# Later first load of Wo and fewer query matmuls ahead of the attention loop

## The chip, the cores and the metric

One core of a Trainium2 chip runs the whole program. The metric is the device time of one execution in microseconds; less is better. A time of several runs is their median.

## The reference

Eight batches of 256 tokens with 512 features go through a gated cross-attention block and a gated mixture-of-experts block:

```python
x = x + tanh(g_xattn[0]) * attention(layernorm(x), ctx_2048, Wq, Wk, Wv, Wsk, Wsv, Wo)
x = x + tanh(g_ffn[0]) * ffn(layernorm(x), router, gate, up, down, amplitudes, expert_scale, shared weights)
# attention: 32 query heads of 16 features, 8 key heads; q = concat(ctx, xn) @ Wq
# k = xn @ Wk and ctx @ Wsk, v likewise; both key sets are masked to a window of 64 positions
# o = softmax(q k^T / 4 + alibi) v, then o @ Wo
```

## The kernel before

Every matrix product is made of three passes, high x high, low x high and high x low, where each operand is split into a rounded part ("hi", made by ScalarE, ACT) and the rest ("lo", made by VectorE, DVE, or GpSimd, POOL). A weight half (128 x 512) arrives in a staging buffer, is rounded (`weights_high`, L1032), and its rest is formed (`weights_low`, L1403 on DVE, L847 on POOL). `wait_split` waits until both parts stand.

Ahead of the loop, TensorE (PE) does batch 0's keys, values and queries (`keys_values`, L1865; `first_queries`, L1896), turns the normalised rows (`prep`, L1845), then batch 1's keys and its first queries (`queries`, L1807). A query product `r` (0 to 3) of a batch has 24 matmuls of 128 x 256.

The loop over slots `n` is software-pipelined by a table of offsets written out by hand. 32 slots make one batch (8 groups of 4 windows). In slot `n`, PE computes the scores of unit `n` (L1921), DVE their maxima (L1448), PE turns the maxima after each 8 slots, and 18 slots later PE computes the scores turned (L1948), ACT their exponentials (L1099). Products with v (L1962), the scaling by POOL (L816), two 32 x 32 transposes by DVE (L1466, L1475) and `o_high` / `o_low` (L1110, L822) bring the attention output to `OT`, which meets `WO` from slot 56 on. Between these, PE gets pieces of later batches' projections.

Queries and keys reach the stacked operands `QS` and `KS` by DMA. Keys are written to DRAM (`keep_k`, L580) and read back (`stack_k`, L596). Queries either go straight from SBUF to SBUF in three DMAs of 64 KB a group (`stack_q_direct`, L603; batches 0, 1 and 7), or to DRAM (`keep_q`, L586) and back in one DMA of 192 KB a group (L619). All of these are issued by the one in-order SP queue, and each slot's waits in it stand in the way of what follows. `scores(4g)` waits for the stacks of group `g`.

SP's order ahead of its loop is: weights and rows, `load_ctx(1)`, `load_x(2)`, `keep_k(0)`, the four loads of Wo (L562), the stacks of batch 0 for eight groups, `keep_k(1)`. `Q1` holds batch 1's queries, in SBUF that the normalised rows `X1N` and the turned rows `XS` use later; Wo is staged where `OT` lies later. The later user of each place waits for the earlier one.

Of the kernel before, what the change touches and what calls it, by code (L numbers as in the profile page):

```python
# [80 lines left out]
LOAD_ROWS, STATS = -61, (-51, -50)  # L81
# [5 lines left out]
EARLY_Q = ((-1, -1, 7), (-1, -1, 8), (9, 10, 11), (12, 13, 14))  # L87
PIECES = 8
# [6 lines left out]
SPLIT_WO = 12  # L95
FIRST_STACK, WARM = 16 * (1 + PARTS), 7
TANH, LOAD_GATES = 54, 44
# [77 lines left out]
def projections():  # L175


    order = [("k", 0, 0), ("v", 0, 0)] + [("q", 0, r) for r in range(G)] + [("k", 1, 0), ("q", 1, 0), ("q", 1, 1)]
# [19 lines left out]
def build(nc, a, out):  # L198
# [27 lines left out]
    wo_stage = at("wo_stage", 184 * KIB, [P, HC, HID])  # L226
    OT = {h: at(f"oT_{h}", (184 + n * 4) * KIB, [P, TB, HC, P], F32R) for n, h in enumerate(("hi", "lo"))}
    Q1 = {h: at(f"second_qT_{h}", (216 - n * 8) * KIB, [P, NB, 2, G, HQ], F32R) for n, h in enumerate(("hi", "lo"))}
# [152 lines left out]
    def staging(n):  # L381
        if n >= FIRST_O:
            return wo_stage[:, n - FIRST_O, :]
        return stage[:, n % 8, :]
# [55 lines left out]
    def straight(b):  # L440


        return b in (1, B - 1)

    def q_loads(b):


        return 16 * sum(PARTS if straight(i) else 1 for i in range(1, b + 1))
# [102 lines left out]
    def _(sp):  # L551
# [60 lines left out]
        def stack_q(b, g):  # L612
            sp.wait_ge(st_mm, (b - 1) * UNITS + NB * (g + 1))
            if straight(b):
# [3 lines left out]
            sp.wait_ge(q_kept, 16 * PARTS * (b - 1))  # L618
# [21 lines left out]
        for n in range(FIRST_O, len(halves)):  # L640
            weight(n)
# [5 lines left out]
        keep_k(1)  # L647
        for n in range(SLOTS):
# [22 lines left out]
            if b is not None:  # L671
# [3 lines left out]
                else:  # L675
                    sp.wait_ge(prep_t, 2 * TB)
# [14 lines left out]
            if s == STACKED[HK - 1] + 2:  # L691
                for g in range(HK):
                    sp.wait_ge(q_in[g], q_loads(B - 1))
# [75 lines left out]
    def _(pool):  # L769
# [259 lines left out]
    def _(act):  # L1029
# [73 lines left out]
        def o_high(p):  # L1103
# [4 lines left out]
            elif c == 0:  # L1108
                wait_split(act, len(halves) - 1)
# [679 lines left out]
    def _(pe):  # L1789
# [476 lines left out]
```

## Time and profile before

| | us |
|---|---|
| median of 3 runs | 892.43 |
| the three runs | 886.06, 892.43, 1215.84 |
| the profiled execution (the last of these values) | 1215.84 |
| its span, first to last instruction | 1213.9 |
| mean granted TensorE clock in it | 0.655 |

The profiled execution is the longest of the three: 323 us above the median. Its span leaves 1.9 us outside. In the profile a share of 99% for PE says that some matmul was always under way, at the clock that was granted; it does not say that PE would be as full at a higher clock.

### The profile page before, as it was taken

The numbers are of one execution on the slowest core, as the hardware profiler recorded it, in microseconds if no ns is written. First come the engines' busy times: TensorE is split into PE (matmuls) and PEld (weight loads), VectorE is DVE, ScalarE is ACT, GpSimd is POOL, SyncE is SP. The second block draws the span as 40 slices with busy tenths as digits, with TensorE's granted clock in tenths as the row PEclk, the third lists the DMA queues.
The fourth block names the chain that finished last, engine by engine and source line by source line (L and its number), as shares of the span: only waits on it lengthen the run. The fifth ranks groups of instructions, "written<-read, shape, count | busy, mean of one in ns | idle before, by whom it ended". The sixth has DMA issues, their size and how long they took to land.

```text
span 1213.9 us, 17380 instructions
## 1 busy us (share of the span) xinstructions
PE 1205.9 (99%) x6662; PEld 910.6 (75%) x6662; DVE 541.2 (45%) x983; ACT 404.0 (33%) x810; POOL 487.1 (40%) x526
## 2 busy tenths in 40 slices
PE   9999999999999999999999999999999999999998
PEld 9999898989898998766666656666666666666665
DVE  6554545554555446311254353434344434443445
ACT  5543343433343335430231223222322233222321
POOL 4532332323223203414484523444555455555320
PEclk7666666666666666666666666666666666666666
DMA  7734454535454336601010333110101101010034
GB/s 236 161 90 118 125 159 118 165 112 166 116 143 144 97 97 163 214 1 35 18 35 18 113 123 131 35 53 18 53 18 53 52 18 52 28 60 18 1 120 158
DMA packets 77947, 110.17 MB, mean 91 GB/s; under 512 B 7329, under 2 KB 49058, under 8 KB 76834
## 3 DMA queue, kind: packets, MB, share of 16 engines
q1 hardware_dynamic: 75656, 108.04, 30.6%
q10 hardware_dynamic: 2210, 1.03, 0.4%
q8 instruction: 53, 0.87, 0.3%
q14 instruction: 28, 0.23, 0.1%
HBM read 71.76 MB, written 32.05 MB: 86 GB/s over the span
## 4 chain that ended last, share of the span: by engine, by line
PE 98%; DVE 1%; issue 0%; ACT 0%; POOL 0%; POOLq 0%
PE ps_scores L2162 21%; PE ps_proj L1807 14%; PE ps_scoresT L2162 10%; PE ps_scoresT L1948 7%; PE ps_proj L1796 7%; PE ps_scores L1796 6%; PE ps_o L1962 6%; PE ps_scores L1921 5%; PE ps_scoresT L1796 5%; PE ps_proj L2162 5%; PE ps_proj L1865 5%; PE ps_o_max L1980 1%; PE ps_o_max L1845 1%; PE ps_scoresT L1896 1%; PE ps_o_max L1796 1%; PE ps_scores L1896 1%
## 5 line engine op out<-in xcount | busy, mean ns | idle before, releaser
L1448 DVE TENSOR_REDUCE neg_max<-ps_scores 128x2 f32<-128x384 f32 (+1 forms) x256 | 132.0, 518 | 218.2 <-PE ps_scores L1921 217.8
L1099 ACT ACTIVATE probsT<-ps_scoresT 128x512 f32<-128x512 f32 (+1 forms) x256 | 138.4, 544 | 248.8 <-PE ps_scoresT L1948 244.3
L1315 ACT ACTIVATE part_sums<-ps_scores 128x512 f32<-128x512 f32 x96 | 57.4, 598 | 232.5 <-PE ps_scores L2162 232.5
L1948 PE MATMUL ps_scoresT<-q_stack,k_stack 116*128 116x256 f32 x448 | 127.5, 358 | 1.3 <-ACT probsT L1099 1.3
L1921 PE MATMUL ps_scores<-k_stack,q_stack 114*128 114x192 f32 (+1 forms) x512 | 115.4, 312 | 1.1 <-DVE neg_max L1448 0.7
L1921 PEld LDWEIGHTS ps_scores<-k_stack,q_stack 114*128 114x128 f32 x512 | 106.1, 248 | 12.4 <-DVE neg_max L1448 2.4
L962 POOL TENSOR_TENSOR w_expert_lo<-w_sums,w_expert_hi 128x256 fp32r<-128x256 f32 x64 | 61.6, 972 | 105.4 <-ACT w_expert_hi L1238 105.4
L816 POOL TENSOR_TENSOR o_normal<-o_blocks,inv_sums 128x256 f32<-128x256 f32 x32 | 19.9, 621 | 201.5 <-DVE inv_sums L1469 201.5
L1948 PEld LDWEIGHTS ps_scoresT<-q_stack,k_stack 116*128 116x128 f32 x448 | 93.5, 249 | 6.9 <-issue 2.3
L974 POOL TENSOR_TENSOR big<-big,basis 128x512 f32<-128x512 f32 x56 | 71.6, 1288 | 41.2 <-DVE basis L1746 41.2
L1962 PE MATMUL ps_o<-probsT,v_ones 128*32 128x128 f32 (+1 forms) x2048 | 77.0, 324 | 0.0
L1807 PE MATMUL ps_proj<-actT_hi,wq_hi 128*128 128x256 f32 x224 | 76.2, 340 | 0.4 <-DVE second_qT_lo L1425 0.4
L1807 PE MATMUL ps_proj<-actT_hi,wq_lo 128*128 128x256 f32 x224 | 76.1, 340 | 0.0
L1807 PE MATMUL ps_proj<-actT_lo,wq_hi 128*128 128x256 f32 x224 | 75.4, 336 | 0.0
L1716 DVE TENSOR_TENSOR part_sums<-part_sums,ps_scoresT 128x512 f32<-128x512 f32 x32 | 22.0, 687 | 114.9 <-ACT part_sums L1315 114.9
L1962 PEld LDWEIGHTS ps_o<-probsT,v_ones 128*32 128x32 f32 x2048 | 64.3, 130 | 11.1 <-issue 0.8
L1737 DVE TENSOR_TENSOR basis<-part_sums,silu_gate 128x512 f32<-128x512 f32 x32 | 22.2, 693 | 106.3 <-ACT silu_gate L1323 106.3
L962 POOL TENSOR_TENSOR w_expert_lo<-w_raw,w_expert_hi 128x256 fp32r<-128x256 f32 x48 | 38.5, 815 | 76.5 <-ACT w_expert_hi L1238 76.5
L822 POOL TENSOR_TENSOR oT_lo<-oT_raw,oT_hi 128x256 fp32r<-128x256 f32 x32 | 23.5, 733 | 113.1 <-ACT oT_hi L1110 113.1
L2162 PE MATMUL ps_scores<-sum_lo,w_expert_hi 128*128 128x512 f32 x128 | 65.1, 508 | 0.0
L2162 PE MATMUL ps_scores<-sum_hi,w_expert_hi 128*128 128x512 f32 x128 | 65.1, 508 | 0.0
L2162 PE MATMUL ps_scores<-sum_hi,w_expert_lo 128*128 128x512 f32 x128 | 65.0, 508 | 0.0
(302 smaller groups left out, 2856.5 us busy)
## 6 DMA issues: line engine op xcount, KB each, us to landing
k_stack<-k_kept SPq DMA_DIRECT2D x64, 192.0 KB, 3.9
big<-coeff_rows SPq DMA_DIRECT2D x8, 1024.0 KB, 4.7
q_stack<-q_kept SPq DMA_DIRECT2D x40, 192.0 KB, 3.9
q_kept<-qT_hi SPq DMA_DIRECT2D x10, 512.0 KB
x_rows<-in_x SPq DMA_DIRECT2D x9, 512.0 KB, 4.8
k_kept<-kT_hi SPq DMA_DIRECT2D x16, 256.0 KB
x_kept<-x_rows SPq DMA_DIRECT2D x16, 256.0 KB, 2.0
w_raw<-in_L_ffn_w_gate SPq DMA_DIRECT2D x16, 256.0 KB, 2.9
```

The source lines that it names most:

```text
L962: pool.tensor_tensor(WS[n % 2]["lo"][:, w, :], w_source(n, w), WS[n % 2]["hi"][:, w, :].bitcast(F32), ALU.subtract).then_inc(e_lo, 1)
L974: pool.tensor_tensor(dst, dst, BS[:, j, :], ALU.add).then_inc(acc_done, 1)
L1099: act.activation(PT[:, g % 2, 2 * j:2 * j + blocks].rearrange("p h f r w -> p (h f r w)"), ST[:, n % 2, 0:blocks].rearrange("p h n -> p (h ...
L1315: act.activation(TP[:, u % 2, j, :], src[:, u % 2, :], ACT.Copy).then_inc(taken, 1)
L1448: dve.tensor_reduce(NM[:, g // 2 % 2, g % 2, 2 * i:2 * i + 2], SA[:, n % 2, :, 0:keys], AX.X, ALU.max, negate=True).then_inc(max_done, 1)
L1796: ins = pe.matmul(out, stat(s, c), mov(m, c), start=c == cs[0] and j == 0, stop=c == cs[-1] and j == PARTS - 1)
L1807: ins = pe.matmul(out, stat(s, c), mov(m, c), start=i == 0, stop=i == len(steps) - 1, skip_group_check=True)
L1865: ins = pe.matmul(dst[:, src * T:(src + 1) * T], WKV[w][:, m + src, c, :], AT[x][:, src * HC + c, :], start=i == 0, stop=i == HC * PARTS - ...
L1921: ins = pe.matmul(SA[:, n % 2, f, 0:2 * (near.stop - near.start)], QS[0:TOP, g, i, f].rearrange("p r w -> p (r w)"), keys[:, near, :].rear ...
L1948: ins = pe.matmul(ST[:, n % 2, v, :], KS[0:ROWS, g, j + v, 1 - v].rearrange("p w s -> p (w s)"), QS[0:ROWS, g, j + v].rearrange("p f r w - ...
L1962: ins = pe.matmul(POB[32 * r:32 * r + 2 * D, n % 2, j * W:j * W + cols_j], VA[:, j, n % HK, :], PT[:, n % 2, 2 * j:2 * j + cols_j // W, :, ...
L2162: ins = pe.matmul(bank[:, u % 2, :], WS[n % 2][s][:, w, c * P:(c + 1) * P], operand(MEETS[w], m, c, g), start=first and c == 0 and j == 0, ...
```

## The change

- Wo: its four loads leave the place ahead of batch 0's stacks. They are issued at slots 24 and 28, into `X1` and a small buffer; the splits move from slots 12 to 15 to slots 34 to 37 (ACT and POOL). The reload of `X1` at slot 42 waits for the split of the first two.
- Batch 1's queries: product 0 has half of its matmuls ahead of the loop (all 24 before) and the rest in slots 1, 3, 5 and 7, three each; product 1 moves from slots 0 to 7 (three each) to slots 9 to 11; products 2 and 3 start at 11 and 13 instead of 9 and 12.
- `Q1` moves to where `OT` lies later. So `o_high` of the first pair (slot 32) waits for the DMAs that read `Q1`, and POOL's first `x1_normalise` no longer does.
- Batch 1's queries go through DRAM for groups 2 to 7 (three writes of 512 KB by `keep_q(1)`, then one read a group), straight only for groups 0 and 1.
- `first_queries` waits for both parts of a weight half and does the three passes of a product in a row, instead of starting on the rounded part and going over the four products in each pass.
- Rows and context of batches 3 to 7 are loaded 3 slots earlier, the gates 6 slots earlier, the tanh 4 slots earlier.

```diff
-LOAD_ROWS, STATS = -61, (-51, -50)
+LOAD_ROWS, STATS = -64, (-51, -50)
-EARLY_Q = ((-1, -1, 7), (-1, -1, 8), (9, 10, 11), (12, 13, 14))
-PIECES = 8
+EARLY_Q = ((-1, -1, 7), (9, 10, 11), (11, 12, 13), (13, 14, 15))
+DIRECT = 2
+EARLY_PIECES = {1: 4, 3: 5, 5: 6, 7: 7}
-SPLIT_WO = 12
+LOAD_WO, SPLIT_WO = (24, 28), 34
-TANH, LOAD_GATES = 54, 44
+TANH, LOAD_GATES = 50, 38
...
-    wo_stage = at("wo_stage", 184 * KIB, [P, HC, HID])
+    wo_stage = at("wo_stage", 216 * KIB, [P, 2, HID])
-    Q1 = {h: at(f"second_qT_{h}", (216 - n * 8) * KIB, ...
+    Q1 = {h: at(f"second_qT_{h}", (184 + n * 4) * KIB, ...
...
-            return wo_stage[:, n - FIRST_O, :]
+            return (X1, wo_stage)[(n - FIRST_O) // 2][:, (n - FIRST_O) % 2, :]
...
-        return b in (1, B - 1)
+        return b == B - 1 or (b == 1 and g < DIRECT)
...
+            if n == FIRST_O:
+                sp.wait_ge(prep_t, 2 * TB)
...
-            sp.wait_ge(q_kept, 16 * PARTS * (b - 1))
+            sp.wait_ge(q_kept, 16 * PARTS * b)
...
         keep_k(0)
-        for n in range(FIRST_O, len(halves)):
-            weight(n)
         for g in range(HK):
             stack_k(0, g)
             stack_q_first(g)
             if g == 4:
                 load_ctx(2)
         keep_k(1)
+        keep_q(1)
...
+            if n in LOAD_WO:
+                for m in range(2):
+                    weight(FIRST_O + 2 * LOAD_WO.index(n) + m)
...
                 else:
-                    sp.wait_ge(prep_t, 2 * TB)
+                    wait_split(sp, FIRST_O + 1)
                 sp.dma_start(X1[:], x_t[:, b]).then_inc(x1_in, 16)
...
-            elif t == 0:
-                for g in range(HK):
-                    pool.wait_ge(q_in[g], q_loads(1))
...
             elif c == 0:
-                wait_split(act, len(halves) - 1)
+                act.wait_ge(q_kept, 16 * PARTS)
+                for g in range(DIRECT):
+                    act.wait_ge(q_in[g], q_loads(1, g))
...
             for c in cs:
-                for j, (w, m) in enumerate((("hi", "hi"), ("hi", "lo"), ("lo", "hi"))):
-                    if j == 0:
-                        pe.wait_ge(weights_hi, HALF_Q[c] + 1)
-                    elif w == "lo":
-                        wait_split(pe, HALF_Q[c])
-                    for r in range(G):
+                wait_split(pe, HALF_Q[c])
+                for r in range(G):
+                    for j, (w, m) in enumerate(PASSES):
...
         queries(1, 0, 0, 2)
         keys_values("k", 1, 1)
-        queries(1, 0, 1, 2)
...
-            if n < PIECES:
-                queries(1, 1, n, PIECES)
+            if n in EARLY_PIECES:
+                queries(1, 0, EARLY_PIECES[n], 8)
```

## Rows read from the trace of the kernel before

**Rows 1.** The page: span, busy time and share of each engine.

```profile
span 1213.9 us, 17380 instructions
PE 1205.9 (99%) x6662; PEld 910.6 (75%) x6662; DVE 541.2 (45%) x983; ACT 404.0 (33%) x810; POOL 487.1 (40%) x526
```

**Rows 2.** Windows: engines' busy us (instructions), granted clock, DMA share, GB/s.

```profile
3.00:4.00 1.00, 1.00 (x4) 0.82 (x3) 0.00 (x0) 0.58 (x1) 0.00 (x0) 1.00 0.98 309
6.00:7.00 1.00, 0.94 (x3) 0.26 (x1) 1.00 (x3) 0.60 (x2) 0.00 (x0) 0.65 1.04 365
...
0.00:41.00 41.00, 39.82 (x223) 37.95 (x223) 23.26 (x43) 22.05 (x41) 24.41 (x34) 0.70 0.71 214
41.00:560.00 519.00, 515.45 (x4440) 462.31 (x4439) 249.19 (x564) 204.86 (x421) 147.10 (x193) 0.65 0.47 125
```

**Rows 3.** Waits of PE over the whole span, two of six kinds: us, times, longest.

```profile
PE ps_scoresT L1948 <- ACT probsT L1099: 1.3, 4, 0.4
...
PE ps_proj L1807 <- DVE second_qT_lo L1425: 0.4, 1, 0.4
```

**Rows 4.** The chain that ended last, in order of time, 35 to 41 us.

```profile
35.33 1.95 PE ps_proj L1807 x12
37.27 1.94 PE ps_proj L1865 x12
39.21 2.00 PE ps_proj L1807 x12
```

**Rows 5.** SP's queue in order of time, 24 to 72 us.

```profile
24.37 0.60 SPq L580 DMA_DIRECT2D k_kept<-kT_lo  x1
25.02 3.49 SPq L562 DMA_DIRECT2D wo_stage<-in_L_xattn_Wo  x4
31.42 0.65 SPq L596 DMA_DIRECT2D k_stack<-k_kept  x1
33.46 0.62 SPq L603 DMA_DIRECT2D q_stack<-qT_hi  x1
...
35.45 0.57 SPq L596 DMA_DIRECT2D k_stack<-k_kept  x1
...
52.62 0.57 SPq L596 DMA_DIRECT2D k_stack<-k_kept  x1
...
71.19 0.57 SPq L596 DMA_DIRECT2D k_stack<-k_kept  x1
```

**Rows 6.** DMA issues by kind: count, KB each, median us to landing.

```profile
xT_kept<-xs_hi SPq DMA_DIRECT2D x5, 512.0 KB, 3.1
...
q_stack<-qT_hi SPq DMA_DIRECT2D x32, 64.0 KB, 3.2
wo_stage<-in_L_xattn_Wo SPq DMA_DIRECT2D x4, 256.0 KB, 6.2
```

**Rows 7.** PE in order of time at the loop's start and in slot 9.

```profile
41.00 0.40 PE L1921 MATMUL ps_scores<-k_stack,q_stack 114*128 114x128 f32 x2
...
48.88 0.38 PE L1807 MATMUL ps_proj<-actT_hi,wq_hi 128*128 128x256 f32 x1 [0.38 <-DVE second_qT_lo L1425]
```

**Rows 8.** Groups of instructions between 7 and 41 us.

```profile
L1403 DVE TENSOR_TENSOR wq_lo<-w_stage,wq_hi 128x512 fp32r<-128x512 f32 x8 | 5.3, 684 | 0.7 <-ACT wq_hi L1032 0.7
```

**Rows 9.** The splits of Wo: engine, count, duration min/median/max.

```profile
L1032 ACT ACTIVATE wo_hi<-wo_stage x4: 619/622/623, 54.0 to 58.9; 128x512 fp32r<-128x512 f32 x4
L847 POOL TENSOR_TENSOR wo_lo<-wo_stage,wo_hi x4: 1274/1280/1283, 54.8 to 65.0; 128x512 fp32r<-128x512 f32 x4
```

**Rows 10.** ACT in order of time around slots 32 to 35.

```profile
80.97 0.41 ACT L1110 ACTIVATE oT_hi<-oT_raw 128x256 fp32r<-128x256 f32 x1
...
86.72 0.60 ACT L1099 ACTIVATE probsT<-ps_scoresT 128x512 f32<-128x512 f32 x1 [2.40 <-PE ps_scoresT L1948]
```

**Rows 11.** POOL in order of time, slot 35.

```profile
88.61 0.62 POOL L816 TENSOR_TENSOR o_normal<-o_blocks,inv_sums 128x256 f32<-128x256 f32 x1 [6.42 <-DVE inv_sums L1469]
```

**Rows 12.** DVE in order of time: slot 1, then slot 37.

```profile
42.28 0.56 DVE L1448 TENSOR_REDUCE neg_max<-ps_scores 128x2 f32<-128x384 f32 x1 [0.42 <-PE ps_scores L1921]
...
91.42 0.44 DVE L1475 STREAM_TRANSPOSE oT_raw<-o_normal 128x256 f32<-128x256 f32 x1
```

More of the change, by code:

```diff
@@ L175, in projections @@
 def projections():
-    order = [("k", 0, 0), ("v", 0, 0)] + [("q", 0, r) for r in range(G)] + [("k", 1, 0), ("q", 1, 0), ("q", 1, 1)]
+    order = [("k", 0, 0), ("v", 0, 0)] + [("q", 0, r) for r in range(G)] + [("k", 1, 0), ("q", 1, 0)]
     for n in range(SLOTS):
@@ L225, in build @@
     stage = at("w_stage", 168 * KIB, [P, 8, HID])
-    wo_stage = at("wo_stage", 184 * KIB, [P, HC, HID])
+    wo_stage = at("wo_stage", 216 * KIB, [P, 2, HID])
     OT = {h: at(f"oT_{h}", (184 + n * 4) * KIB, [P, TB, HC, P], F32R) for n, h in enumerate(("hi", "lo"))}
-    Q1 = {h: at(f"second_qT_{h}", (216 - n * 8) * KIB, [P, NB, 2, G, HQ], F32R) for n, h in enumerate(("hi", "lo"))}
+    Q1 = {h: at(f"second_qT_{h}", (184 + n * 4) * KIB, [P, NB, 2, G, HQ], F32R) for n, h in enumerate(("hi", "lo"))}
     OB = at("o_blocks", 192 * KIB, [P, 2, T // 32, 2 * D])
@@ L438, in queries_of, with straight, q_loads @@
         return Q1 if b == 1 else Q
-    def straight(b):
-        return b in (1, B - 1)
-    def q_loads(b):
-        return 16 * sum(PARTS if straight(i) else 1 for i in range(1, b + 1))
+    def straight(b, g):
+        return b == B - 1 or (b == 1 and g < DIRECT)
+    def q_loads(b, g):
+        return 16 * sum(PARTS if straight(i, g) else 1 for i in range(1, b + 1))
     def wait_rows(eng, g):
@@ L613, in stack_q @@
             sp.wait_ge(st_mm, (b - 1) * UNITS + NB * (g + 1))
-            if straight(b):
+            if straight(b, g):
                 sp.wait_ge(pj_done, passed("q", b, G - 1))
@@ L692, in _ @@
                 for g in range(HK):
-                    sp.wait_ge(q_in[g], q_loads(B - 1))
+                    sp.wait_ge(q_in[g], q_loads(B - 1, g))
                 router = cols(a["L0_ffn_w_router"], 0)
@@ L1077, in q_high @@
             elif b >= 3 and r == 0:
-                act.wait_ge(q_kept, 16 * PARTS * (b - 2))
+                act.wait_ge(q_kept, 16 * PARTS * (b - 1))
             act.wait_ge(q_mm, G * b + r + 1)
@@ L1889, in first_queries @@
             for c in cs:
-                for j, (w, m) in enumerate((("hi", "hi"), ("hi", "lo"), ("lo", "hi"))):
-                    if j == 0:
-                        pe.wait_ge(weights_hi, HALF_Q[c] + 1)
-                    elif w == "lo":
-                        wait_split(pe, HALF_Q[c])
-                    for r in range(G):
+                wait_split(pe, HALF_Q[c])
+                for r in range(G):
+                    for j, (w, m) in enumerate(PASSES):
                         ins = pe.matmul(place("q", 0, r)[:, 0:T], WQ[w][:, c, r * P:(r + 1) * P], AT[m][:, c, :],
-                                        start=c == 0 and j == 0, stop=c == 2 * HC - 1 and j == PARTS - 1,
-                                        skip_group_check=True)
-                        if c == 2 * HC - 1 and j == PARTS - 1:
-                            ins.then_inc(q_mm, 1)
+                                        start=c == 0 and j == 0, stop=c == 2 * HC - 1 and j == PARTS - 1)
+                    if c == 2 * HC - 1:
+                        ins.then_inc(q_mm, 1)
         def turn_v(b):
@@ L1914, in scores @@
                 if b >= 1:
-                    pe.wait_ge(q_in[g], q_loads(b))
+                    pe.wait_ge(q_in[g], q_loads(b, g))
             if n >= 2:
@@ L2073, in _ @@
                     b = queries_due(n, r, part)
-                    if b is not None and (b > 1 or r > 1):
+                    if b is not None and (b, r) != (1, 0):
                         queries(b, r, part)
```

## The prediction

> **What bounds the kernel now.** I read the page's busy times first, then the windows with the granted clock, then PE's waits, and only then the timelines of the first 95 us, where the change works. PE is busy 1205.9 of 1213.9 us [rows 1]. The clock was granted in full at 3 to 4 us and at 0.65, between the two levels of 1.2 and 2.4 GHz, from 6 us on, and it stayed there through the loop [rows 2]. PE's waits inside the loop are counted in tenths of a microsecond [rows 3]. So this execution is bound by matmuls at 0.65 of the clock, and every supply chain hides behind them.
>
> The median run is another matter. The profiled execution is 1215.84 us, the other two are 886.06 and 892.43, and the median is the latter. PE's work scaled to a full clock is an estimate of 1205.9 x 0.655 = 790 us. A run of 889 us (the mean of those two) is then one of two things: PE at the full clock with some 99 us of waits that the profile doesn't show, or PE always full at 790 / 889 = 0.89 of the clock. I keep both readings. In either, PE's stretches shrink to 0.655 or 0.74 of what the profile shows, while DMA, ACT, DVE and POOL keep their durations. What is slack here may be a wait there.
>
> **The change part by part.**
>
> *Matmuls.* None is added or removed. Twelve go from ahead of the loop into it: 12 for 2.00 us at the profile's clock [rows 4], so 1.3 us at full clock.
>
> *Wo's loads.* After the last write of K (issued until 24.97) SP issues four loads for 3.49 us, and the first stack of keys, which waits for K to land, goes out at 31.42, 6.4 us after K's last issue. Group 0's queries follow at 33.46, when they are evicted [rows 5]. Wo's 1 MB lands in 6.2 us a piece [rows 6] and shares the DMA engines with K's write. Without it a write of comparable size lands in 3.1 us [rows 6], so K lands about 3.3 us earlier; the bounds are 0 (the write was slow by itself) and 3.9 us, to the time at which nothing but a landing of 2.5 us were left. By the Trainium skill, DMA: Bandwidth & Descriptors, Anatomy of one DMA, a DMA costs about 2.0 us plus its bytes over 436 GB/s; for 768 KB that is an estimate of 3.8 us, and the gain by it would be 2.6 us. In the profiled execution none of this shows, because group 0's stacks land at about 35.4 + 3.2 = 38.6 and PE comes to the loop at 41.00 [rows 5 to 7]. Scaled to the full clock it does: I estimate from the same rows that the first queries end near 26 us, K lands near 28.7, group 0's last query DMA is issued near 31.3 and lands near 34.5, while PE has filler only to about 33. So PE waits about 1.5 us at the loop's start before the change. After it, K lands near 25.5, the queries' eviction near 27 becomes the late one (the last product is then the only one left to evict, since each is finished in turn), and the stacks land near 32, with PE's filler ending at 31.7. The loop starts 2.3 us earlier.
>
> *The moved matmuls in the loop.* From its start the loop is bound in that scaled reading by SP: eight groups take 52.62 - 31.42 = 21.2 us to issue, 2.8 to 3.0 us a group [rows 5], and four slots of scores with three matmuls each take 3.3 us at the profile's clock and 2.2 at full. The 12 added matmuls find this gap and cost 0; with the gap gone they cost 1.3 us. A slot of scores alone is held by its maximum, 0.56 us [rows 12], so even slots without filler lose up to 0.2 us each, 4 x 0.2 = 0.8 us. I take 0.3 for both together.
>
> *Order of the first queries.* Each half now waits for its lo part, 0.68 us later than the hi part [rows 8]; eight halves bound it at 5.5 us, and 0 is the other bound. PE afterwards waits for DVE's rows and splits anyway, which the order doesn't move, so I take 0 to 0.5, and 0.2 for the sum. At the profile's clock it is 0: PE arrives later than the lo parts.
>
> *Waits in the slots 32 to 37.* The Wo splits are 4 x 0.62 us on ACT and 4 x 1.28 us on POOL [rows 9]. In slots 12 to 15 nothing hung on them. In slots 34 to 37 ACT has its exponentials, and behind POOL's first two splits stands the scaling of the second pair, 0.62 us at 88.61 [rows 11], for which DVE waits at 91.42 [rows 12], with the maxima queued behind it, and PE's scores behind those. From ACT's 86.72 + 0.60 [rows 10], a chain of 0.62 + 2 x 1.28 + 0.62 = 3.8 us ends at 91.1 in the profile, just in time. The distance to 91.42 shrinks from 4.1 us to 2.7 to 3.0 at the higher clock, so DVE would be late by about 1 us, and the two score buffers take some of it: 0.6 us, bounds 0 and 2.5. Before that, `o_high` at 80.97 [rows 10] waits for group 1's direct queries: they are released at 71.19 [rows 5], need 2.5 us of issue and 3.2 us to land [rows 6], so about 77; at the higher clock the 9.8 us shrink to 6.4 and the 5.8 do not. No wait, bound 1 us.
>
> *The rest.* `keep_q(1)` adds 1.5 MB of writes and stands on SP behind nothing urgent: the next entry of the queue is slot 22. Six groups then need one DMA in place of three, which frees SP by 12 x 0.58 us in slots 30 to 50; PE waits for none of them before, so it is worth 0. Were `keep_q(1)` late, group 2 at slot 30 would be the first to feel it, ten slots ahead of its use. Loading rows and context 3 slots earlier, the gates and the tanh: their consumers wait for nothing in the profile, 0. PE's only wait for an early query, 0.38 us in slot 9 [rows 7], goes, but product 2 in slot 11 takes the bank of product 0, which is now finished in slot 7: 0.
>
> The sum: -2.3 + 0.3 + 0.2 + 0.6 = -1.2 us. At the profiled execution's own clock the sum is 0 + 0.3 - 0.4 = 0, so 1215.8 again. Against the other two runs, whose mean is 889.2, it gives 888.0. This is below what a measurement of this kernel can tell: the two runs differ by 0.7% and I take 2% as the line between a change and none.
>
> **The rivals.**
>
> *More is gained.* In the shorter runs the first 50 us may be paced by SP and the DMA engines throughout: the share is 0.71 over the first 41 us even with PE at 0.65 [rows 2]. Then Wo's 3.49 us of issue and its 6.2 us in the engines come off whole, about 9.7 us: 879. Against it: DVE's chain and PE's own work stand beside it.
>
> *It does nothing.* If PE is full at 0.89 of the clock, slack covers the stacks nearly everywhere, and the time is 889 give or take 1.
>
> *Slower by blocked splits.* POOL's four splits in slots 34 to 37, 5.1 us, and ACT's 2.5 us delay the output chain and with it DVE and PE. It is dearer than the early gain if more than 2.9 us of it reach PE. The whole of 7.6 us would give 889.2 - 1.7 + 7.6 = 895.1. For it speaks the bare 0.3 us of margin at the profile's clock; against it that it occurs once, not in each batch.
>
> *The clock.* Slots 0 to 8 become sparser in matmuls. In the profile the clock fell to 0.65 while PE was busy and did not rise again [rows 2], so it follows something other than idle time there. If it halved for the roughly 5 us of these slots, the cost is 5 us: 893. The Trainium skill (TensorE: Matmul & The Clock Gate, HAM oscillation) has idle gaps bring the half rate; no row here shows that.
>
> **How the numbers follow.** Forecast 0.56; more gained 0.10; nothing 0.16; slower by splits 0.14; clock 0.04. The predicted time is 888. The range reaches down to 886.06 less the 8 us of most of the larger gain, 878, and up to 892.43 plus the full 7.6 us, 900. Faster by over 2% would need 17.8 us, more than all terms together: 0.03. Slower by over 2%: 0.03. Within: 0.94.
>
> **What would show it.** Right: the last K write and the first stack of keys lie about 3 us apart instead of 6.4, the first scores start 2 us earlier in the profile (39 against 41.00), the maxima in slots 0 to 8 stand closer together than 0.8 us, DVE's transpose in slot 37 shows an idle time ended by POOL, and PE's share stays at 98 or 99% at any clock of 0.65. Wrong: a PE wait of several microseconds at a score or a turned score after slot 34, or K's write still at 6 us. A clock that differs from run to run would move the time more than all of this.

## The result and the profile after

The changed kernel takes 894.47 us (median of 7 runs, 892.60 to 894.64), the kernel before 888.65 us (median of 7). The ratio is 1.0058, its 95% interval 1.0035 to 1.0081: slower by 5 to 6 us, inside 2%, and resolved all the same. The ratios leave out the executions of the kernel before that ran far longer at a low mean clock (1215.84 us here, 1067.66 and 1422.68 us beside e0 to e3). The forecast was 888.0 us in 878 to 900. The range held the time; the direction was wrong.

The profile of before stood at a clock of 0.655. A second profile of the unchanged kernel, taken on the chip of the first experiments, was granted the full clock (885.15 us, span 883.2) and is the base of every comparison below; the profiled execution of after took 892.44 us. The page after (the first row answers to [rows 1]):

```profile
span 890.4 us, 17369 instructions
PE 872.0 (98%) x6662; PEld 758.9 (85%) x6662; DVE 539.8 (61%) x983; ACT 400.1 (45%) x810; POOL 509.9 (57%) x526
```

At nearly the full clock PE is still busy 98% of the span, 872 us, not the 790 us that the prediction scaled to. So PE is nearly full at either clock, and time is won or lost in the few places where PE stops or its clock is halved. They are found by the start of the same slot's scores in the two traces. The table is worked out from the first matmul of L1921 in each slot: the first row is the time in us in the second profile of before, each other row the distance to it. Experiments are named by their number.

```
slot            0      8     16     30     34     36     96    232    240   span
before      34.62  40.54  49.23  63.45  69.48  73.20 158.90 352.35 359.82  883.2
after       -2.22  -1.73  +1.73  +1.27  +2.18  +3.74  +3.74  +3.74  +7.09  890.4
e1          -2.16  -3.27  -0.70  -1.13  +2.83  +3.02  +3.02  +3.02  +6.58  889.9
e2          -1.26  -2.45  -1.91  -1.89  +4.60  +4.65  +4.65  +4.65  +6.10  890.7
e3          -1.13  -1.91  +0.33  -0.12  +5.94  +5.95  +5.94  +5.95  +7.39  890.8
e4          -1.15  -2.61  -0.09  -0.52  +4.45  +4.59  +4.59  +4.60  +8.12  891.4
e5          +0.84  +1.23  +1.23  +1.25  +1.26  +1.26  +1.26  +1.28  +4.63  887.9
e6          -1.02  -0.66  +1.28  +0.86  +6.39  +6.48  +7.33  +7.34 +10.24  893.5
e7          +0.49  +0.57  +0.57  +0.58  +9.11  +9.11  +9.11  +9.13 +10.57  893.9
e8          -0.74  -1.92  -1.40  -1.31  +1.87  +1.90  +1.90  +1.91  +1.94  885.2
e9          -1.23  -2.17  -1.88  +1.21  +1.22  +1.22  +1.22  +1.23  +1.24  884.6
e10         -1.78  -2.90  -0.62  +0.18  +0.22  +0.25  +1.10  +1.11  +1.11  884.5
e11         -1.80  -2.49  -0.14  +0.08  +0.33  +0.33  +0.33  +0.34  +3.16  886.5
e12         +0.87  +1.26  +1.25  +1.24  +1.25  +1.25  +1.25  +3.02  +3.07  886.4
e13         +0.76  +0.60  +0.37  +0.37  +0.37  +0.37  +0.37  +4.38  +5.83  891.4
e14         -1.62  -2.33  -0.40  -0.85  +4.16  +4.23  +4.23  +6.00  +6.05  889.3
e15         -1.26  -2.18  +0.11  -0.32  +6.03  +6.54  +6.55 +10.56 +12.01  897.8
```

Each row is one execution, and rows that should be alike show how far one can be trusted. Up to slot 101 e12 and e13 are the kernel before, and they come to the loop 0.87 and 0.76 us later than the base. Up to slot 24 e1, e4, e6, e14 and e15 do the same work as after: they start between -2.16 and -1.02 (after: -2.22) and stand between -1.13 and +0.86 at slot 30 (after: +1.27). A difference of up to 1.2 us at slot 0, or 2.4 us at slot 30, between two single rows shows nothing by itself. Nor is the profiled execution always the typical one: that of e8 is the fastest of its 13, those of e5 and e15 are the slowest of 12 and 5.

The row of after reads: 2.2 us won at the loop's start; 3.5 us lost in slots 8 to 16; 2.5 us lost in slots 30 to 36; then nothing at all for 196 slots; and 3.35 us lost between slots 232 and 240, in the last batch, whose work the change doesn't touch.

**The start.** SP's queue, the kernel before (full clock), then after (both answer to [rows 5]; columns are start, duration, queue and line, operation):

```profile
22.11 0.61 SPq L580 DMA_DIRECT2D k_kept<-kT_lo  x1
22.77 3.80 SPq L562 DMA_DIRECT2D wo_stage<-in_L_xattn_Wo  x4
29.43 0.65 SPq L596 DMA_DIRECT2D k_stack<-k_kept  x1
30.18 0.62 SPq L603 DMA_DIRECT2D q_stack<-qT_hi  x1
```

```profile
21.81 0.61 SPq L583 DMA_DIRECT2D k_kept<-kT_lo  x1
27.46 0.64 SPq L599 DMA_DIRECT2D k_stack<-k_kept  x1
28.20 0.62 SPq L606 DMA_DIRECT2D q_stack<-qT_hi  x1
```

From the end of K's last issue (22.72, 22.42) to the first stack of keys it is 6.7 us before and 5.0 us after. So Wo's loads had cost K's write 1.7 us, about half of the 3.3 us taken. This figure is steady: 6.7 to 7.1 us in the five profiles that have the loads there, 4.9 to 5.1 us in the twelve that don't. PE comes to the loop 2.2 us earlier all the same, in these two profiles and by the means of like ones (35.2 us in e0, e5, e7, e12 and e13; 33.0 us in after, e1, e4, e6, e14 and e15).

**Slots 30 to 36.** SP's queue in after, from `keep_q(1)` on:

```profile
52.25 0.75 SPq L589 DMA_DIRECT2D q_kept<-second_qT_hi  x1
53.04 0.57 SPq L589 DMA_DIRECT2D q_kept<-second_qT_lo  x1
53.66 0.65 SPq L589 DMA_DIRECT2D q_kept<-second_qT_hi  x1
58.03 0.59 SPq L599 DMA_DIRECT2D k_stack<-k_kept  x1
59.13 0.66 SPq L606 DMA_DIRECT2D q_stack<-second_qT_hi  x1
59.84 1.35 SPq L606 DMA_DIRECT2D q_stack<-second_qT_lo  x1
61.23 2.21 SPq L606 DMA_DIRECT2D q_stack<-second_qT_hi  x1
63.55 1.24 SPq L565 DMA_DIRECT2D x_rows<-in_L_xattn_Wo  x2
64.89 0.57 SPq L599 DMA_DIRECT2D k_stack<-k_kept  x1
65.56 0.55 SPq L606 DMA_DIRECT2D q_stack<-second_qT_hi  x1
66.16 0.58 SPq L606 DMA_DIRECT2D q_stack<-second_qT_lo  x1
66.79 0.58 SPq L606 DMA_DIRECT2D q_stack<-second_qT_hi  x1
67.41 1.05 SPq L565 DMA_DIRECT2D wo_stage<-in_L_xattn_Wo  x2
```

The three writes are issued in 2 us. Behind them stand batch 1's first stacks, and they are late in two ways. The issues of queries take 0.66, 1.35 and 2.21 us for the first group here. In the second profile of before they take 0.58 us each for the first group, and once 1.23 us for the second:

```profile
60.70 0.58 SPq L603 DMA_DIRECT2D q_stack<-second_qT_hi  x1
61.34 0.58 SPq L603 DMA_DIRECT2D q_stack<-second_qT_lo  x1
61.96 0.58 SPq L603 DMA_DIRECT2D q_stack<-second_qT_hi  x1
...
63.94 1.23 SPq L603 DMA_DIRECT2D q_stack<-second_qT_lo  x1
```

And they land late. The landing rows of the tile `q_stack` between 58 and 69 us are, of before:

```profile
DMA to landing us min/median/max: 2.3/3.0/4.4
```

(as in [rows 6]) and of after:

```profile
DMA to landing us min/median/max: 4.8/6.1/7.5
```

The keys' stacks go from a median of 3.9 to 8.1 us in the same windows. Group 1's last read closes at 73.4, and `o_high` hangs on it, with an exponential behind it and a product with v behind that. ACT in time, then the chain that ended last:

```profile
69.53 0.60 ACT L1101 ACTIVATE probsT<-ps_scoresT 128x512 f32<-128x512 f32 x1 [2.39 <-PE ps_scoresT L1948]
73.52 0.42 ACT L1114 ACTIVATE oT_hi<-oT_raw 128x256 fp32r<-128x256 f32 x1 [3.40 <-DMA q_stack<-second_qT_hi]
73.84 0.37 ACT L1101 ACTIVATE probsT<-ps_scoresT 128x256 f32<-128x256 f32 x1
```

```profile
66.79 6.63 DMA q_stack<-second_qT_hi
...
73.52 0.10 ACT oT_hi L1114
...
73.84 0.38 ACT probsT L1101
...
74.26 0.97 PE ps_o L1962 x32
```

In the second profile of before `oT_hi` stands at 67.85 with no wait at all, as in [rows 10].

**The clock.** Windows, of before at full clock, then of after (columns: window, its length, busy us and instructions of PE, PEld, DVE, ACT, POOL; granted clock, DMA share, GB/s; they answer to [rows 2]):

```profile
35.00:40.00 5.00, 4.09 (x35) 3.88 (x35) 3.29 (x7) 4.97 (x11) 5.00 (x6) 1.00 0.66 141
70.00:75.00 5.00, 5.00 (x94) 4.91 (x87) 2.84 (x6) 2.14 (x4) 0.62 (x1) 1.00 0.61 142
350.00:355.00 5.00, 3.84 (x58) 3.50 (x62) 3.66 (x10) 3.24 (x8) 4.04 (x4) 1.00 0.91 242
355.00:360.00 5.00, 4.71 (x71) 4.06 (x59) 3.81 (x9) 3.48 (x8) 0.62 (x1) 1.00 1.02 241
```

```profile
35.00:40.00 5.00, 3.79 (x24) 3.21 (x24) 3.37 (x10) 4.84 (x10) 4.91 (x6) 0.88 0.60 116
40.00:45.00 5.00, 5.00 (x35) 5.00 (x35) 2.73 (x7) 0.27 (x1) 0.00 (x0) 0.78 0.85 224
70.00:75.00 5.00, 3.67 (x79) 3.41 (x80) 1.19 (x3) 1.50 (x5) 0.73 (x1) 1.00 1.07 208
355.00:360.00 5.00, 3.55 (x22) 3.15 (x26) 3.71 (x8) 2.76 (x7) 2.77 (x3) 0.63 0.77 198
360.00:365.00 5.00, 4.95 (x77) 4.33 (x70) 2.22 (x5) 1.46 (x3) 0.00 (x0) 0.69 0.74 186
```

Taken in steps of 1 us, after spends 3.4 us at half clock (1.2 GHz) from 38 to 43 us and 6.8 us from 356 to 364; the second profile of before spends none. What PE did before the first fall: two waits, 0.66 us for a maximum at 34.13 and 1.21 us for group 1's first queries at 36.65. Slots 8 to 16 have this fall in them, and the moved matmuls: PE does 72 query matmuls between the scores of slots 8 and 16, 48 in the kernel before, and 12 instead of 24 between those of slots 0 and 8 (both are taken apart below).

### The profile page after: what moved, and what is told of

The parts are those of the page before. It is cut to its first block, busy times and chain, and to the rows that moved or that the text cites. A ratio compares the mean times of both kernels' runs of the same rounds, so it can differ in the third digit from the quotient of the medians.

```text
span 890.4 us, 17369 instructions
## 1 busy us (share of the span) xinstructions
PE 872.0 (98%) x6662; PEld 758.9 (85%) x6662; DVE 539.8 (61%) x983; ACT 400.1 (45%) x810; POOL 509.9 (57%) x526
## 4 chain that ended last, share of the span: by engine, by line
PE 89%; DVE 3%; DMA 3%; issue 1%; SPq 1%; POOL 1%; ACT 1%; DVEq 0%; POOLq 0%; ACTq 0%
PE ps_scores L2161 20%; PE ps_proj L1811 13%; PE ps_scoresT L2161 10%; PE ps_scoresT L1948 6%; PE ps_scores L1800 6%; PE ps_o L1962 6%; PE ps_proj L1800 5%; PE ps_scores L1921 5%; PE ps_scoresT L1800 5%; PE ps_proj L2161 5%; PE ps_proj L1869 4%; DMA xn_rows<-in_x 1%; DMA q_stack<-second_qT_hi 1%; DVE neg_max L1452 1%; PE ps_o_max L1980 1%
## 5 line engine op out<-in xcount | busy, mean ns | idle before, releaser
L1948 PE MATMUL ps_scoresT<-q_stack,k_stack 116*128 116x256 f32 x448 | 106.8, 311 | 1.7 <-ACT probsT L1101 1.6
L1921 PE MATMUL ps_scores<-k_stack,q_stack 114*128 114x192 f32 (+1 forms) x512 | 97.1, 273 | 6.0 <-DVE neg_max L1452 4.0
L1921 PEld LDWEIGHTS ps_scores<-k_stack,q_stack 114*128 114x128 f32 x512 | 82.6, 193 | 13.5 <-DVE neg_max L1452 4.7
L1948 PEld LDWEIGHTS ps_scoresT<-q_stack,k_stack 116*128 116x128 f32 x448 | 70.5, 192 | 6.4 <-ACT probsT L1101 2.8
L1811 PE MATMUL ps_proj<-actT_hi,wq_lo 128*128 128x256 f32 x224 | 63.4, 284 | 0.0
L1962 PE MATMUL ps_o<-probsT,v_ones 128*32 128x128 f32 (+1 forms) x2048 | 57.5, 265 | 1.3 <-ACT probsT L1101 1.3
L1750 DVE TENSOR_TENSOR basis<-basis,big 128x512 f32<-128x512 f32 x56 | 56.8, 1015 | 1.0
L1962 PEld LDWEIGHTS ps_o<-probsT,v_ones 128*32 128x32 f32 x2048 | 51.8, 112 | 5.2 <-ACT probsT L1101 1.5
L2161 PE MATMUL ps_scores<-xnT_hi,w_expert_hi 128*128 128x512 f32 x128 | 49.8, 389 | 0.0
L2161 PE MATMUL ps_scores<-xnT_hi,w_expert_lo 128*128 128x512 f32 x128 | 49.8, 389 | 0.0
```

The source lines that it names most:

```text
L1750: dve.tensor_tensor(dst, BS[:, j, :], cB[:, k % 2, group_columns(t)], ALU.mult).then_inc(basis_done, 1)
L1811: ins = pe.matmul(out, stat(s, c), mov(m, c), start=i == 0, stop=i == len(steps) - 1, skip_group_check=True)
L1921: ins = pe.matmul(SA[:, n % 2, f, 0:2 * (near.stop - near.start)], QS[0:TOP, g, i, f].rearrange("p r w -> p (r w)"), keys[:, near, :].rear ...
L1948: ins = pe.matmul(ST[:, n % 2, v, :], KS[0:ROWS, g, j + v, 1 - v].rearrange("p w s -> p (w s)"), QS[0:ROWS, g, j + v].rearrange("p f r w - ...
L1962: ins = pe.matmul(POB[32 * r:32 * r + 2 * D, n % 2, j * W:j * W + cols_j], VA[:, j, n % HK, :], PT[:, n % 2, 2 * j:2 * j + cols_j // W, :, ...
L2161: ins = pe.matmul(bank[:, u % 2, :], WS[n % 2][s][:, w, c * P:(c + 1) * P], operand(MEETS[w], m, c, g), start=first and c == 0 and j == 0, ...
```

## The experiments

Four jobs, each a set of runs on one chip: e0 to e3; e5 to e8; e4 with e9 to e11; e12 to e15. Each ratio is to runs of the kernel before in the same job.

**e0: the kernel before, unchanged.** 

> The kernel before, unchanged, to have its profile at a clock near the 0.994 at which the changed kernel was profiled. Expected 886 to 891 us. Theory (the wait for group 1's direct queries is the loss): in slots 24 to 32 ACT's first oT_hi waits for no DMA, and the stretch from the first score to slot 40 is 3 to 5 us shorter than in the changed kernel. Rival (the loss is at the loop's start): the first score of slot 8 is reached earlier than 38.9 us. Third possibility (the steady batches lose through the earlier loads of rows): the loss builds up evenly, batch by batch.

885.15 us, clock 1.000. It is the base described above.

**e1: one direct group instead of two.**

```diff
-DIRECT = 2
+DIRECT = 1
```

> The changed kernel with only group 0 of batch 1 stacked straight from SBUF, so that the first oT_hi in slot 32 waits for a DMA released four slots earlier. Theory (that wait costs 3 to 5 us): 0.4 to 0.6% faster than the changed kernel, so a ratio to before of 1.000 to 1.002, and oT_hi's wait of 3.4 us on the DMA is gone. Rivals (loop start, or rows loaded earlier, or splits in slots 34 to 37): ratio to before stays at 1.005 to 1.007.

893.09 us, 1.0056 [1.0034, 1.0078]: as slow as the change. `o_high`'s wait is gone, and PE now waits for the same jam at a score, in the waits of PE from 60 to 85 us:

```profile
PE ps_scores L1921 <- DMA k_stack<-k_kept: 2.4, 1, 2.4
```

So the wait of `o_high` was the last to end, but a stack of batch 1 stood right behind it.

**e2: batch 1's early query products as before.**

```diff
-EARLY_Q = ((-1, -1, 7), (9, 10, 11), (11, 12, 13), (13, 14, 15))
-EARLY_PIECES = {1: 4, 3: 5, 5: 6, 7: 7}
+EARLY_Q = ((-1, -1, 7), (-1, -1, 8), (9, 10, 11), (12, 13, 14))
+PIECES = 8
...
```

> The changed kernel with the early query matmuls where the kernel before has them. Theory of the DMA wait in slot 32: the ratio to before stays at 1.004 to 1.007. Rival that the matmuls moved out of slots 0 to 7 leave PE idle there: 0.2 to 0.5% faster than the changed kernel, a ratio of 1.001 to 1.004.

893.74 us, 1.0070 [1.0048, 1.0092]. At slot 30 it is 0.8 us ahead of e1 (-1.89 against -1.13) and 1.0 to 2.8 us ahead of e4, e6, e14 and e15, so the moved matmuls cost 0.8 us at the least. All of it, and more, is lost at slot 32, where PE waits 3.9 us for `k_stack`.

**e3: the order of the first queries as before** (three passes over four products, starting on the rounded part).

> The changed kernel with the first queries in the order of before (starts on the hi part, passes outermost). Theory of the DMA wait: the ratio to before stays at 1.004 to 1.007. Rival that waiting for the lo parts delays the start: 0.1 to 0.2% faster than the changed kernel. By my forecast's term (0.2 us) nothing measurable; it could also be slower by 0.1%, since the four evictions then come together.

893.88 us, 1.0066 [1.0046, 1.0086]. The loop starts at -1.13. That is 1.1 us behind after, but inside the -2.22 to -1.02 of the six profiles that have the new order, so no gain or cost of the order is shown. PE waits 3.6 us for `k_stack` at slot 32, ACT 2.4 us for the direct reads.

**e4: rows and context loaded 3 slots later, as before.**

```diff
-LOAD_ROWS, STATS = -64, (-51, -50)
+LOAD_ROWS, STATS = -61, (-51, -50)
```

> The changed kernel with the rows and contexts loaded at their old slots. In the steady batches the distance to before is constant, so I expect no effect there. Batch 3's rows and context no longer join the queue at slot 32: if that adds to the jam, the ratio falls by 0.001 to 0.002; else it stays at 1.004 to 1.007.

893.25 us, 1.0047 [1.0021, 1.0073]; the wait at slot 32 is still 2.4 us for `k_stack`. In e4 and in after the distance is constant from slot 36 to 232, with late and with early loads: they are worth nothing, as forecast.

**e5: the kernel before with only the new order of the first queries.**

> The kernel before with only the new order of the first queries. Theory (each product ends in turn, so three of its four evictions are done when the last one ends, and the first stacks leave SP earlier): the first score comes 1.0 to 1.2 us earlier than the 34.62 us of before, the time falls by 1 us at equal mean clock, a ratio of 0.997 to 1.000. My forecast's term (waiting for the lo parts costs 0.2 us): the first score 0 to 0.3 us later and a ratio of 1.000 to 1.002.

887.72 us, 0.9995 [0.9976, 1.0014]. It gains nothing. The loop starts at +0.84, but so it does at +0.87 and +0.76 in e12 and e13, whose order is that of before; the order's effect is smaller than this spread.

**e6: the changed kernel with Wo's loads past the stacks of groups 0 and 1.**

```diff
-LOAD_WO, SPLIT_WO = (24, 28), 34
+LOAD_WO, SPLIT_WO = (36, 38), 42
```

> The changed kernel with the loads of Wo at slots 36 and 38 and their splits at 42 to 45. Theory A (Wo's 1 MB in slots 24 to 28 is what makes the stacks of slot 32 late): the waits for DMA around slot 32 fall below 0.5 us and slot 40 lies 3 us earlier relative to before than in the changed kernel; ratio 0.999 to 1.003. Theory B (the 1.5 MB that keep_q(1) writes in slots 17 to 20 block the SP queue and the DMA engines): a wait of 1.5 to 4 us at slot 32 stays, and the ratio is 1.004 to 1.006. Both together: the wait is halved.

893.18 us, 1.0066 [1.0040, 1.0092]. With Wo's 1 MB out of the way PE still waits 2.9 us for `k_stack` at slot 32. The theory that Wo's loads jam the stacks falls. Another 0.85 us goes between slots 36 and 96, where the loads and splits of Wo now lie; e10, which has two of the loads and splits there, loses as much.

**e7: the kernel before, plus the writes of `keep_q(1)`, which nothing reads.** Direct reads of all groups stay; the counts of `q_kept` move by one batch, and POOL's first reuse of `Q1`'s place waits for the writes too.

```diff
...
         keep_k(1)
+        keep_q(1)
...
```

> The kernel before plus the three writes of batch 1's queries to DRAM, which nothing reads; the stacks stay straight. It doubles the suspected cost alone. Theory B: SP's issues of batch 1's first stacks take over 1 us each in place of 0.58, PE or ACT waits 1 us or more for a stack at slot 32, the clock falls there in some runs, and the time is 2 to 5 us above before (1.002 to 1.005). Theory A: nothing over 1 us at slot 32, ratio 1.000 to 1.002.

896.43 us, 1.0100 [1.0076, 1.0125]. The jam appears in the kernel before, and stronger. SP's queue, PE in time, and the landings of `q_stack` from 58 to 69 us:

```profile
57.93 2.67 SPq L586 DMA_DIRECT2D q_kept<-second_qT_hi  x1
...
62.19 1.46 SPq L603 DMA_DIRECT2D q_stack<-second_qT_hi  x1
63.70 2.39 SPq L603 DMA_DIRECT2D q_stack<-second_qT_lo  x1
66.14 1.90 SPq L603 DMA_DIRECT2D q_stack<-second_qT_hi  x1
```

```profile
73.63 0.66 PE L1923 MATMUL ps_scores<-k_stack,q_stack 114*128 114x128 f32 x2 [6.19 <-issue]
```

```profile
DMA to landing us min/median/max: 3.8/6.5/7.4
```

The profile names no releaser for the 6.19 us, but the instruction is `scores(32)`, the first that needs group 0 of batch 1. Between slots 30 and 36 8.5 us are lost, part of them at half clock (71 to 79 us).

**e10: the changed kernel without `keep_q(1)`.** All groups read `Q1` directly, so it stays at its old place, and Wo comes through `X1` in two pairs (loads at slots 24 and 36, splits at 34, 35, 42, 43).

```diff
-DIRECT = 2
+DIRECT = HK
-LOAD_WO, SPLIT_WO = (24, 28), 34
+LOAD_WO, SPLIT_AT = (24, 36), {34: 12, 35: 13, 42: 14, 43: 15}
...
-        keep_q(1)
```

> The changed kernel without the writes of keep_q(1): batch 1's queries lie at their old place and all eight groups are stacked straight; Wo is loaded in two pairs into X1 at slots 24 and 36, split at 34, 35, 42, 43. If those writes are what costs the time at slot 32, no wait for a stack is left there and slot 64 is 2 to 4 us earlier than in the changed kernel, level with before or up to 1 us later: ratio 0.999 to 1.003. If Wo's loads or the splits in slots 34 to 37 cost it, the ratio stays above 1.004.

888.31 us, 1.0007 [0.9987, 1.0026], level with before. There is no wait for a stack at slot 32; the landings of `q_stack` from 58 to 69 us are nearly those of before, and the first three issues of queries take 0.59, 0.59 and 0.52 us:

```profile
DMA to landing us min/median/max: 2.2/3.7/4.5
```

The rest of the change is in it, and it gains nothing either: -1.78 at slot 0 is +0.14 by slot 20. Of this 1.9 us go between slots 12 and 16, as in every profile with the moved matmuls and in none without them (PE has 40 query matmuls there in place of 24), and 0.8 us by slot 20, where PE waits 0.96 us for the queries of group 5 of batch 0.

**e8: the kernel before with the new order of first queries, Wo's loads moved behind batch 0's stacks** (still ahead of `keep_k(1)`; splits at slots 24 to 27).

```diff
-        for n in range(FIRST_O, len(halves)):
-            weight(n)
         for g in range(HK):
...
+        for n in range(FIRST_O, len(halves)):
+            weight(n)
         keep_k(1)
```

> The kernel before, with the new order of the first queries and with the four loads of Wo moved behind the first stacks (ahead of keep_k(1)), split in slots 24 to 27; batch 1's queries stay straight from their old place, so no writes are added. If the early gain is real and the loss lies in the added traffic of slots 17 to 28, the first score comes 1.3 us earlier than in before, slot 30 2.5 us earlier, and slot 64 still 2 us earlier: 2 us faster at equal clock, ratio 0.995 to 0.999. If Wo's loads disturb wherever they lie near slot 32, slot 64 is level with before or later.

891.14 us, 1.0041 [1.0025, 1.0057]. It leads by 1.3 us at slot 30 and loses 3.2 us there: POOL's splits of Wo stand in front of the low part of the turned context, and PE waits for it and for two exponentials behind it; the clock is halved from 66 to 70 us. The profile is of the fastest execution, 887.20 us at a mean clock of 0.998; the other twelve took 890.56 to 892.37 us at 0.990 to 0.994, so a good part of what the median lost isn't in it (waits of PE, 60 to 85 us):

```profile
PE ps_scoresT L1944 <- ACT probsT L1099: 1.2, 2, 0.9
PE ps_proj L1865 <- POOL actT_lo L809: 1.1, 1, 1.1
```

**e9: e8 with one load of Wo behind each stack of groups 3 to 6, splits at 18.**

```diff
...
+            if 3 <= g < 7:
+                weight(FIRST_O + g - 3)
...
```

> As e8, with the four loads of Wo set between the stacks of groups 3 to 6 and the splits in slots 18 to 21, clear of POOL's work in slots 27 and 28. In e8 slot 30 was 2.2 us ahead of before and slot 34 0.5 us behind, with POOL's context low part 1.1 us late and the splits ahead of it. If the splits' place was the reason, slot 64 stays 1.5 to 2.5 us ahead: 2 us faster at equal clock, ratio 0.996 to 0.999. If not, the loss at slots 31 to 34 stays, ratio 1.000 to 1.004.

887.83 us, 0.9996 [0.9978, 1.0014]. The lead of 1.87 us at slot 24 is gone by 28, in a wait of 1.17 us for DVE's maxima and a half clock from 58 to 62 us.

**e11: e9 with the moved query matmuls.** 

> As e9, with the early query matmuls where the changed kernel has them. From the changed kernel with them undone (slot 30 was 2.7 us ahead of before in place of 1.1 or less) I expect the first score 1 us earlier than in e9 but slot 30 1 to 2 us later, and PE idle in slots 0 to 7: ratio 0.001 to 0.003 above e9.

886.94 us, 0.9993 [0.9977, 1.0009]. The moved matmuls cost 1.3 us by slot 24 (-0.57 against -1.87); by the medians it is no slower than e9.

Then what was left: why does the last batch lose 3.35 us, and only in some runs? In the second profile of before PE waits there for the same maxima (2.7 us in all from 345 to 370 us, the longest 1.1) and stays at full clock. Two theories: it depends on where in time the batch falls (P), or on what the changed kernel did early (H). Extra matmuls at slot 101, in the full part of the loop, shift everything behind them and touch nothing else (they write scores that the following matmul overwrites).

```diff
-            for f in range(2):
+            for f in (0,) * (16 if n == 101 else 0) + (0, 1):
```

**e12: before, 16 extra.** 

> The kernel before with 16 extra matmuls in slot 101 (each writes the scores' half again that the next one overwrites, so nothing else changes); a pair of them takes about 0.2 us, so everything behind shifts by 1.6 us. Theory P (position: the half clock in the last batch hangs only on where that batch falls in the run): the last batch falls to half clock in some or most runs, mean clock 0.994 to 0.998, time before + 1.6 + up to 3.3 us. Theory H (history: it hangs on what the changed kernel does early): clock as in the kernel before in the same job, time + 1.6 us.

889.17 us, 1.0011 [0.9993, 1.0029]; shift 1.77 us, last batch +0.05, clock 0.996 to 1.0 in ten runs.

**e13: before, 36 extra.** 

> The kernel before with 36 extra matmuls in slot 101, a shift of 3.6 us, the size of the changed kernel's distance there (3.74). Theory P: half clock in the last batch as in the changed kernel, time + 3.6 + 3.3 = 6.9 us at a mean clock near 0.994. Theory H: clock as before, time + 3.6 us.

893.30 us, 1.0051 [1.0035, 1.0067]; shift 4.01 us, last batch +1.45 by slot 240 and 1.4 us more by slot 255, clock 0.995 to 1.0.

**e14: after, 16 extra.** 

> The changed kernel with the same 16 extra matmuls. Theory P: the last batch falls at another place, so its half clock may go: time + 1.6 - 3.3 us against the changed kernel. Theory H: half clock stays, time + 1.6 us, mean clock 0.992 to 0.994.

893.62 us, 1.0066 [1.0043, 1.0088]; last batch +0.05, clock 0.990 to 0.998. It does 1.8 us more work than after and its median isn't above after's 894.47, but its ten runs spread from 891.39 to 900.28.

**e15: after, 36 extra.** 

> The changed kernel with the same 36 extra matmuls. Theory P: as for 16, clock different from 0.992 to 0.994, which would show as a time other than + 3.6 us. Theory H: half clock stays, time + 3.6 us against the changed kernel, about 898.

895.43 us, 1.0075 [1.0049, 1.0100]; last batch +1.45 by slot 240 and 1.4 us more by slot 255, clock 0.991 to 0.998. Against after it is +1.0 us for 4.0 us more work, not the +3.6 of theory H.

Waits of PE in the last batch, 345 to 370 us, in e14, where the clock doesn't fall:

```profile
PE ps_scores L1921 <- DVE neg_max L1452: 1.9, 4, 1.1
PE ps_scoresT L1936 <- DVE max_halves L1462: 0.5, 1, 0.5
```

In e15, where it falls, the same two rows read 1.4 us and 0.5 us, with the same longest waits of 1.1 and 0.5. So the waits are alike, and the fall comes or doesn't. Over all 17 profiles the step from slot 232 to 240 takes one of three sizes: 0 to 0.1 us (six profiles, of before, e8, e9, e10, e12 and e14), 1.4 to 1.5 (e2, e3, e7, e13, e15) or 2.8 to 3.6 (after, e1, e4, e5, e6, e11). Three of the middle class (e2, e13, e15) lose another 1.4 us by slot 255, at half clock again. The first class holds the kernel before and the changed one with 16 extra matmuls, and the distance at slot 232 doesn't sort them: e5 (+1.28) falls and e9 (+1.23) doesn't. So H is refuted as the sole cause, and P in its simple form, where a given shift decides, isn't confirmed. What decides in a single execution stays open.

## Why the prediction was wrong

**What bounds the kernel.** Of the two readings kept, PE full at any clock is the nearer: 872 us busy at 0.994. The estimate of 790 us was wrong: PE is busy 867.5 us in the second profile of before at the full clock, 0.72 of the 1205.9 us and not 0.655. With it falls the clock of 0.89 that was put beside it; the runs of before that took 884.57 to 893.74 us were granted 0.992 to 1.0. With so little idle time a few microseconds of stop are the whole matter, and that part of the reasoning held.

**Wo off the queue, -2.3 us at the loop's start.** Right in its sum: -2.22, and the same by the means of like profiles. The parts fit less well. K's write got 1.7 us faster, not 3.3. What gives the other half microsecond isn't shown: the order of the first queries, costed at +0.2, makes no difference that stands out of the spread (e3, e5). The sign that I named, 3 us from K's write to its stack, would have shown this: it reads 5.0. The Trainium skill (DMA: Bandwidth & Descriptors, Anatomy of one DMA) had given an estimate of 3.8 us for the landing and 2.6 us for the gain, by a fit that it states for DMAs issued by GpSimd; here SP issues them, and the trace shows about 5.0 and 1.7.

**The moved matmuls, +0.3, bounds 1.3 and 0.8.** Undersized. I had twelve matmuls added to a loop with gaps at every group. In fact slots 0 to 7 lose twelve and slots 8 to 15 get 24 more, and the 16 of these that lie in slots 12 to 15 cost their full 0.12 us each (1.94 us). Over the whole stretch the cost is at least 0.8 us (e2 against e1, slot 30) and 1.3 us (e11 against e9, slot 24). After itself stands 2.4 us behind e1 at slot 30, with the same matmuls. Of this 1.5 us are there at slot 8 already, ahead of any fall of the clock; most of it is the wait of 1.21 us for group 1's first queries at 36.65, which e1 doesn't have. The other 0.9 us come in slots 8 to 16 (3.46 against 2.57; e4, e6, e14 and e15 lose 1.9 to 2.5 there), where after runs 3.4 us at half clock and the others don't. That is the rival of the clock in its place, at 0.9 to 1.5 us instead of 5; it was given 0.04.

**The Wo splits in slots 34 to 37, +0.6, and the rival that they block (895.1).** Wrong mechanism, though its time was the nearest. ACT's four lie between exponentials, POOL's two before the scaling end in time, and DVE waits 0.93 us:

```profile
77.09 2.55 POOL L849 TENSOR_TENSOR wo_lo<-x_rows,wo_hi 128x512 fp32r<-128x512 f32 x2 [2.34 <-ACT wo_hi L1034]
79.60 0.62 POOL L821 TENSOR_TENSOR o_normal<-o_blocks,inv_sums 128x256 f32<-128x256 f32 x1
```

```profile
80.25 0.45 DVE L1479 STREAM_TRANSPOSE oT_raw<-o_normal 128x256 f32<-128x256 f32 x1 [0.93 <-POOL o_normal L821]
```

The first rows are those of [rows 9] and [rows 11] after, the last that of [rows 12]. The idle time that I named as the sign is there, but the maxima behind it don't hold PE: the distance is +3.74 at slot 36 and at 48. The cost is 0. A forecast of the right size by a wrong cause is worth nothing to the next kernel.

**"`keep_q(1)` adds 1.5 MB of writes and stands on SP behind nothing urgent".** This is the step that failed. I looked at what stands in front of it and at the next entry of the queue (slot 22), and asked whether the writes would be late for their own reader. I didn't ask what happens to the transfers issued behind them. Those, batch 1's first stacks, come four to five microseconds later, are issued at up to 2.21 us each and land in 6.1 us instead of 3.0. The same mistake is in **"No wait, bound 1 us"** for `o_high`: it took 3.2 us of landing from a stretch with no such writes, and the real one took 6.63; the wait was 3.40 us. Taking the writes away makes the changed kernel level (e10), adding them to the kernel before makes it 1.0% slower (e7), and undoing anything else leaves 0.5 to 0.7% (e1 to e4, e6) and moves the wait between `o_high` and the stacks. This is shown. A PE wait of several microseconds at a score was the sign of failure that I named. It came, by this cause, in the experiments (2.4 to 3.9 us at slot 32 in e1 to e4 and e6), two slots ahead of where I had put it; in the changed kernel's own profile PE's longest stop there is 1.33 us, behind `o_high` and its exponential.

**The kept gain.** Even without the writes nothing is left of the 2 us. In e8 to e11 the lead is given back before slot 36: in e10 and e11 mostly to the moved matmuls in slots 12 to 16, in e10 also to a stack at slot 20, in e8 to POOL's low part, in e9 to DVE's maxima and a fall of the clock behind them. This I had not weighed: the forecast carried the whole lead through to the end.

**The clock.** After ran at 0.992 to 0.994 in all eight executions; the kernel before, on the chips of the later experiments, mostly at 0.996 to 1.0 (4 of 26 at 0.994 or less in the last job). At the same mean clock, 0.994, the twelve runs of before beside the experiments take 889.57 to 890.99 us and the three of after 892.44, 892.60 and 894.47; at 0.992 four of before take 891.32 to 893.74 and five of after 893.02 to 894.64. By the medians 2.3 and 2.6 us of the loss are there at equal clock, and some 3 us are the lower clock. So the rival of the clock (893) came near in time as well; it looked for the fall in slots 0 to 8 alone, and most of it lies in the last batch. The runs come from different chips, so the split is rough. A fall in the first 80 us is in the profile of every kernel that has the kept writes (38 to 43 us in after; between 66 and 79 in e1 to e4, e6, e7, e14, e15), each behind a stop of PE. Of kernels without them e0, e10, e11 and e13 show none, and e5, e8, e9 and e12 show one. The Trainium skill (TensorE: Matmul & The Clock Gate, HAM oscillation), which the prediction set aside because no row showed it, has idle gaps bring the half rate, and these falls agree in kind. Two things speak against it as a full account: the last batch, where the same waits bring the fall in one execution and not in the next, and the first profile of before, at 0.65 with PE busy 99% of the span.

**Sums.** Three steps of the working don't come out, none of which moves the forecast. The terms ahead of the splits add to -1.8, not -1.7, so blocked splits would give 895.0 and would be dearer than the gain from 1.8 us on, not 2.9. The sum at the profile's own clock is -0.1, not 0. And 52.62 - 31.42 = 21.2 us spans seven groups, from the first stack to the eighth, at 3.0 us a group.

**The other rivals.** That the change does nothing had the right idea of a full PE, but PE's stops weren't covered. That more is gained (879) asked for a start that SP and the DMA engines pace throughout; the lead never passed 3.3 us (e1, slot 8).

No version beats the kernel before: the best, e11 and e9, are level with it inside their intervals.

## What to carry to other kernels

A bulk write is costed not only by its own deadline but by what is issued and what must land in the ten microseconds behind it, with landing times taken from a stretch that has a like load. In a loop where PE is 98% busy, an early lead is worth only what every later supply chain lets through; follow it to the next wait before it is put into the sum. And where a profile fell at another clock than the median, take no PE time from it by scaling. Before a difference between two single profiles is called an effect, see how far profiles of kernels differ that are alike up to that point.

## What the hardware showed

- Three writes of 512 KB from SBUF to DRAM, issued in 2 us, slow the DMAs behind them on the same queue: the first three issues of queries take 0.66, 1.35 and 2.21 us instead of 0.58 (1.46, 2.39 and 1.90 us in e7), reads of 64 KB land in 6.1 us instead of 3.0, stacks of keys in 8.1 instead of 3.9. The DMA share is 0.63 to 0.85 from 58 to 66 us and above 1.0 only from 66 us on; in the kernel before it is 1.17 from 52 to 54 us, and PE's longest wait from 50 to 60 us is 0.5 us, so a high share alone isn't the harm.
- The half clock comes in stretches of 3.4 or 6.8 us, after stops of PE of 1 us or so as well as after 6 us. In the last batch a stretch of 3.4 us costs 1.45 us, one of 6.8 us 2.8 to 3.6 us; in the full part of the loop, slots 36 to 232, none was seen in any of the 17 profiles near the full clock. The first profile of before is unlike them all: 0.65 from 6 us to its end.
- 16 extra matmuls of 192 columns cost 1.77 us and 36 cost 4.01 us, 0.11 us each, and this shift is unchanged 130 slots later: there is no slack to take it.
